# Dividing attention probabilities by their row sums before they are transposed, in a float32 decoder layer on one core

## The reference

```
x = layernorm(x + attention(x))      # 16 heads of 32, softmax over 256 keys, q/k/v/o weights, small 32x32 down/up matrices
x = layernorm(x + x * scan(ctx*ctx)) # scan along the tokens: r = decay*r + ctx*ctx, one decay a head
x = layernorm(x + down(silu(gate(x)) * up(x)))   # hidden 2048; all three weights are splines of few control points
```

```
scores = q @ k.T                              # 256 x 256
p = exp(scores - rowmax) ; rowsum = sum(p)
y = (p / rowsum) @ v
out = concat(y) @ Wo.T
```

## Time and profile before

| | |
|---|---|
| time, median of 3 runs | 684.98 us |
| the profiled execution's own time | 685.51 us |
| its span, first to last instruction | 683.7 us |
| TensorE clock granted, mean | 0.995 |
| PE busy | 656.8 us (96%) |
| DVE busy | 449.5 us (66%) |
| ACT busy | 347.7 us (51%) |
| POOL busy | 294.3 us (43%) |

### The profile page before, as it was taken

One profiled execution on the slowest core, in us unless ns is written; L12 is line 12 of the kernel. 1 busy time (PEld: TensorE's weight loads), 2 busy tenths in 40 slices (PEclk: granted clock), 3 DMA queues, 4 the chain that ended last, 5 costly groups with the idle time before them and its releaser, 6 DMA issues.

```text
span 683.7 us, 12025 instructions
## 1 busy us (share of the span) xinstructions
PE 656.8 (96%) x4312; PEld 533.8 (78%) x4312; DVE 449.5 (66%) x826; ACT 347.7 (51%) x1002; POOL 294.3 (43%) x351
## 2 busy tenths in 40 slices
PE   9999999999999999999988799999999999999993
PEld 9597887878888788788865577888888888888883
DVE  3567687698686877878778688666544555354434
ACT  5566546637466565656667556552334233333230
POOL 1764486886638767594674836100100001000103
PEclk9999999999999999999999999999999999999997
DMA  9621020030220311121112672741193317340301
GB/s 329 221 80 62 1 87 7 2 125 1 94 62 2 133 52 32 63 72 41 40 65 47 159 173 72 210 105 40 35 239 78 81 32 198 72 101 0 124 1 61
DMA packets 22010, 58.06 MB, mean 85 GB/s; under 512 B 4032, under 2 KB 7232, under 8 KB 21056
## 3 DMA queue, kind: packets, MB, share of 16 engines
q1 hardware_dynamic: 16720, 44.45, 22.5%
q0 software_dynamic: 4944, 12.32, 5.9%
q10 hardware_dynamic: 288, 0.52, 0.2%
HBM read 32.11 MB, written 8.39 MB: 59 GB/s over the span
## 4 chain that ended last, share of the span: by engine, by line
PE 78%; DVE 12%; ACT 6%; issue 2%; POOL 1%; DVEq 0%; POOLq 0%; ACTq 0%
PE bank L303 19%; PE bank L305 18%; PE bank L304 18%; PE bank L490 6%; ACT probs L665 5%; PE bank L478 4%; DVE recurrence_T L896 4%; PE bank L512 4%; DVE minus_max L821 3%; PE bank L1191 2%; PE bank L1096 2%; DVE probsT L835 2%; PE bank L529 1%; PE bank L316 1%; PE bank L498 1%
## 5 line engine op out<-in xcount | busy, mean ns | idle before, releaser
L665 ACT ACTIVATE probs<-bank,minus_max 128x256 f32<-128x256 f32 x256 | 117.3, 486 | 23.8 <-DVE minus_max L821 23.8
L303 PE MATMUL bank<-down,hidden_hi_lo 128*128 128x512 f32 x256 | 100.7, 393 | 1.5 <-DVE hidden_hi_lo L1402 1.5
L305 PE MATMUL bank<-down,hidden_hi_lo 128*128 128x512 f32 x256 | 100.5, 392 | 0.0
L304 PE MATMUL bank<-down,hidden_hi_lo 128*128 128x512 f32 x256 | 100.0, 391 | 0.0
L821 DVE TENSOR_REDUCE minus_max<-bank 128x2 f32<-128x512 f32 x128 | 79.3, 681 | 16.3 <-PE bank L478 16.3
L1398 DVE TENSOR_TENSOR hidden<-bank,silu 128x512 f32<-128x512 f32 x64 | 44.1, 689 | 60.9 <-PE bank L305 58.9
L1356 ACT ACTIVATE silu<-bank 128x512 f32<-128x512 f32 x64 | 38.3, 598 | 82.2 <-PE bank L305 81.3
L1402 DVE TENSOR_TENSOR hidden_hi_lo<-hidden,hidden_hi_lo 128x512 fp32r<-128x512 f32 x64 | 45.5, 711 | 40.9 <-ACT hidden_hi_lo L1369 40.8
L490 PE MATMUL bank<-ident,probs 128*128 128x128 f32 x512 | 65.5, 275 | 6.2 <-ACT probs L665 5.9
L1476 POOL TENSOR_TENSOR ffn_var_eps<-ffn_mean_var,constants 128x4 f32<-128x4 f32 x3 | 0.6, 196 | 156.5 <-DVE ffn_mean_var L1418 156.5
L490 PEld LDWEIGHTS bank<-ident,probs 128*128 128x128 f32 x512 | 56.6, 141 | 14.2 <-ACT probs L665 12.0
(11 more groups left out here) (170 smaller groups left out, 1610.8 us busy)
## 6 DMA issues: line engine op xcount, KB each, us to landing
features_by_group<-features_by_cell SPq DMA_DIRECT2D x128, 128.0 KB, 2.4
ctx_squared_T<-in_ctxT SPq DMA_DIRECT2D x8, 512.0 KB, 3.3
xres<-in_x SPq DMA_DIRECT2D x8, 512.0 KB, 4.6
x_in<-x SPq DMA_DIRECT2D x16, 256.0 KB, 3.1
x_residual<-x POOLq DMA_DIRECT2D x4, 1024.0 KB, 8.1
out_x<-x_residual POOLq DMA_DIRECT2D x16, 256.0 KB, 2.8
xin_T<-in_xT SPq DMA_DIRECT2D x7, 512.0 KB, 3.9
x<-x_rows SPq DMA_DIRECT2D x7, 512.0 KB, 4.1
```

Of the source, the lines that this page charges most:

```text
L303: nc.tensor.matmul(out, wh, xh, start=first, stop=False)
L304: nc.tensor.matmul(out, wh, xl, start=False, stop=False)
L305: return nc.tensor.matmul(out, wl, xh, start=False, stop=last)
L665: inc(nc.scalar.activation(probs[:, g, t, :], S[g][:, t * T:(t + 1) * T], ACT.Exp, bias=nmax[:, g, t:t + 1], accum_out=rsum[:, t, g:g + 1] ...
```

## The change

1. The probabilities are divided in rows, right after exp. `dve_inverse` now takes the reciprocal of one head's two row sums as soon as that head's exp is done. ACT multiplies the probabilities of heads 0 to 2 by it in place (six instructions a stage, at the end of `act_exp`), DVE those of head 3 (`dve_weigh`, two instructions). `pe_t` waits for these and not for exp. The spread reciprocal, its transposes (`pe_r`), the copy `Rb`, and the multiplication of y are gone.
2. y stays in MI: ACT rounds it from there to the high part (between exp of heads 2 and 3 of the next stage), DVE subtracts for the low part of every group. GpSimd's share of that is gone.
3. `pe_s` of the next group stands before `pe_pv` of this one.
4. DVE's order in a stage changes, as shown below; the scan of a batch is split into two halves (groups 2 and 3), and batch 7's moves behind the batches, into the transition. `dve_size` moves as well.
5. In the transition, one job more (four, not three) is done ahead of the FFN, recurrence transposes and `act_rs1` come later, and the first FFN step has one job and not two.
6. The last block's normalisation is done by ACT as x*rstd + (-mean*rstd), with GpSimd computing the bias, and SyncE issues the four output DMAs.

The core of the diff:

```diff
@@ pe_t
         for g in range(HG):
-            pe.wait_ge(s["exp"], 32 * b + 8 * m + 2 * g + 2)
+            if g < ON_ACT:
+                pe.wait_ge(s["pna"], ON_ACT * (4 * b + m) + g + 1)
+            else:
+                pe.wait_ge(s["pnv"], (HG - ON_ACT) * (4 * b + m) + g - ON_ACT + 1)
@@ pe_batch, as at every group
-        pe_r(pe, b, 1)
         pe_k(pe, b, 3, rest)
         pe_extra(pe, b, 1)
+
+        pe_s(pe, b, 2)
         pe_pv(pe, b, 1)
-
-        pe_s(pe, b, 2)
@@ act_exp
         for g in range(HG):
+            if m and g == HG - 1:
+                act_yh(act, b, m - 1)
             act.wait_ge(s["max"], 16 * b + 4 * m + g + 1)
             ...
+        for g in range(ON_ACT):
+            act.wait_ge(s["rinv"], 4 * (4 * b + m) + g + 1)
+            for t in range(TT):
+                last = nc.scalar.activation(probs[:, g, t, :], probs[:, g, t, :], ACT.Copy, scale=rinv[:, g, t:t + 1])
+            inc(last, "pna")
@@ dve_y, and dve_yl gone
-        inc(nc.vector.tensor_tensor(y[:], MI[:, 0:T], Rb[:], ALU.mult), "yv")
+        dve.wait_ge(s["yh"], 4 * b + m + 1)
+        inc(nc.vector.tensor_tensor(yT[1][:, m, :], MI[:, 0:T], yT[0][:, m, :].bitcast(F32), ALU.subtract), "yl")
@@ new in DVE
+    def dve_inverse(dve, b, m, g):
+        dve.wait_ge(s["exp"], 32 * b + 8 * m + 2 * g + 2)
+        inc(nc.vector.reciprocal(rinv[:, g, :], rsum[:, g, :]), "rinv")
+
+    def dve_weigh(dve, b, m):
+        for g in range(ON_ACT, HG):
+            dve.wait_ge(s["rinv"], 4 * (4 * b + m) + g + 1)
+            for t in range(TT):
+                last = nc.vector.tensor_scalar(probs[:, g, t, :], probs[:, g, t, :], rinv[:, g, t:t + 1], None, ALU.mult)
+            inc(last, "pnv")
@@ transition, DVE
+            for q, out in enumerate((B_, C_, A_, B_)):
+                dve_fl(dve, 0, q, out)
             dve_job(dve, 2 * NG, X)
+            dve_scan(dve, B - 1, range(KT))
             dve_r1(dve, B - 1, 0)
             dve_job(dve, 2 * NG + 1, X)
+            dve_stats(dve, B - 2, 1)
             dve_r1(dve, B - 1, 1)
             dve_job(dve, 2 * NG + 2, X)
+            dve_job(dve, 2 * NG + 3, X)
@@ end, SyncE
+            for t in range(BT):
+                sp.wait_ge(s["yout"], BT * (NB - 1) + t + 1)
+                inc(sp.dma_start(out_v[:, BT * (NB - 1) + t, :], res[:, t, :]), "last", 16)
```

223 lines of the change are left out of this document (99 added, 124 removed), and 6 rows, old and new, of the table names.

## The result

The changed kernel takes **723.16 us** in the median (four runs, 720.13 to 724.3), beside 685.26 for the kernel before on the same chip: a ratio of 1.0545 (95% interval 1.0528 to 1.0561), 38 us slower. The forecast was 700, with a range of 687 to 709: the side was right, the size was not.

What follows compares the result with a forecast made beforehand. PE set the pace before; after the change VectorE's queue would bind stages 0, 2 and 3, plus batch 7's wait. Terms 6.0 + 1.5 + 0.5 + 6.5 + 2.5 - 2.1 = +14.9 us took 685.0 to 700, range 687 to 709.

Steps and rivals of the forecast that it cites:

- the chain of a stage: Each stage, from its scores' start S: exps end at S+5.8, then the scalings; stage 0 of batches 2 to 7 takes 11.55 us.
- Stage 2 of batch 7: The size reduction there waits for GpSimd ahead of the copies; next scores at S+14.9, the largest single loss expected, 3.9 us.
- stages 2 and 3 of batches 4 to 6: VectorE's scans between its scalings and copies set these stages: 11.15 and 11.75 us, within +6.0 for the three batches.
- step 1: Batches 0 to 3: VectorE's scalings at 0.4 us busy, 0.3 from start to start; +0.5 for batch 0, +1.5 for 1 to 3.
- Rival C: VectorE's scalings are held up by GpSimd, 0.26 us an instruction in 21 stages: +11, 711 us; chance 0.09.
- step 2: ScalarE's six scalings of each stage start 0.30 us apart; stage 1 takes 10.7 with a wait of 0.2 for head 2.
- The condition that I wrote down for it: Sign of a wrong forecast: ScalarE's scalings at 0.45 us, so that PE waits before its transposes, 0.9 a stage.
- step 3: Transition from stage 3's scores in batch 7: VectorE's later queue delays the first down product to S+31.4; +2.5 us net.
- the tail: Last block's normalisation on ScalarE and outputs issued one by one: -2.1 us, bounds -0.9 and -3.3.
- A: PE still sets the pace in all stages: -7.0 for the removed transposes, -2.1 at the end, 676 us; chance 0.12.
- B: Only batch 7 and the transition lose, batches 0 to 6 come out even: +8, 692 us; chance 0.18.
- D: Gains and losses over the whole kernel cancel and 685 us stands; chance 0.03.

## Why the prediction was right or wrong

**Right: the side, the chain of a stage, and its place in stage 0 and in batch 7.** Exps end at S+5.7 (forecast 5.8). Stage 0 with VectorE's statistics behind the scalings is 11.46 (11.55), and it falls to 10.46 when the statistics go ahead of them. Stage 2 of batch 7, with the size reduction behind ScalarE's and GpSimd's queues, is 15.41 (14.9), and the wait for it 5.12 (over 4). PE waited before the scores of stage 1, released by VectorE's copies, but 0.93 and not 1.8.

**Right by luck: stages 2 and 3 of batches 4 to 6.** The forecast put them down to VectorE's queue, 11.15 and 11.75; they are 11.04 and 11.99 in batch 5. But they stay so without VectorE's scalings (11.04, 11.99) and with the scans ahead of them (11.04, 11.98), and fall without ScalarE's (10.70, 11.21). So ScalarE's pace set them. A wrong reason gave nearly the right lengths, and the +6.0 for these batches, measured +7.7, is near in part by this luck.

**Failed step 1, the price of VectorE's scalings in batches 0 to 3.** Forecast +0.5 and +1.5, measured +7.4 and +10.8: 16.2 of the 23.4 us missed. 3.7 of them are the clock (2.8 in batch 0, 0.9 in batch 1, below). I took VectorE's scaling at 0.4 busy and 0.3 from start to start in all batches, although had a mean of 558 ns for L830, whose undisturbed copy takes 295. The runs: without VectorE's scalings batches 0 to 3 take 48.17 and 136.87 instead of 50.77 and 144.17, and about 7.6 of that difference is left when the dips of both executions are set aside. With GpSimd's two kinds of work cut, batches 1 to 3 take 138.5. Rival C named this mechanism and was given 0.09, with 0.26 us excess per instruction. The excess is 0.56 us where GpSimd works (1.73 for a pair instead of 0.61) and 1.0 at worst (2.57), it takes the scans too, and it falls on the batches that I had declared cheapest. My argument against it, that GpSimd waits at those times, holds in stage 0 of batches 2 to 7 and is wrong in stage 2, where GpSimd splits x and multiplies rows. As a sole cause rival C would be wrong too: it is one of two limits. The remaining 5 or so of the 16.2 belong to ScalarE's share, step 2. In batch 0, where no output product covers the chain, stage 0 is 8.66 without divisions and 11.03 with ScalarE's, whether VectorE's are there or not (two executions without a dip in it); the forecast had no term for that.

**Failed step 2, ScalarE's pace.** 0.30 from start to start came from a copy without a scale in the middle of other work; measured 0.40. The forecast had stage 1 at 10.7, with a wait of 0.2; it is 11.0 without VectorE's part, and 11.57 with eight scalings. The condition that I wrote down for it, 0.45 and a wait ahead of the transposes, came out as a stretch between them (2.67 instead of 1.91), which PE's own waits hardly show (11.0 us over the whole run) and those of its weight load do (42.5 us, 90 times).

**Failed step 3, the transition: +2.5 against +10.1.** The path that I followed, VectorE and TensorE up to the first down product, was right: it starts 33.15 after the scores, where I had 31.4, and at 31.50 in the run with throwaway transposes, whose clock there is 0.89 and not 0.57. What I left out is GpSimd's queue of transfers. The size reduction moved one group later, and the makers stand behind it: from silu 10 to silu 20 after takes 53.00, before 47.45, and with the transfers ahead 47.87. So of the 7.6 missed 5.1 are these transfers and 1.7 the clock; 0.8 stay open.

**Missed: the clock.** No term had it. TensorE at 0.50 to 0.84 cost 2.8 us in batch 0 and 0.9 in batch 1 of the profiled execution, and up to 2.7 behind stage 3's scores in batch 7.

**Undersized: the tail.** -3.5 against -2.1, just outside its bounds of -0.9 and -3.3. The sum took the landing of a transfer as equal, whoever starts it; in the traces the last one landed 3.1 us after GpSimd's start and 2.1 after SyncE's. And -1.8 in the FFN from shifted addresses, for which the kernel before gave no sign.

**Rivals A, B and D** fell. A named the work that goes (7.0 for the transposes): without divisions batches 0 to 6 are 10.7 us shorter than before. How much of that is the transposes and how much the earlier scores, no run separates; the divisions cost four times as much. B and D had batches 0 to 6 even; they lost 25.9.

## What to carry to other kernels

When a small amount of TensorE's work, here a pair of transposes a stage, is replaced by element work on two other engines, price that work in two ways: the mean with a busy neighbour, not the undisturbed duration, and the start-to-start time of a run of the same instruction. Remove suspects singly and together; if the two single gains do not add up to the joint one, each hides a part of the other. And when an instruction moves, follow what stands behind it in every queue it shares with others, the transfers on GpSimd and ScalarE's copies included. A stage that comes out as forecast is no proof of its reason: here stages 2 and 3 came out near the forecast for another reason.

## What the runs showed of the hardware

- VectorE's tensor_scalar of 128x256 in SBUF takes 0.34 to 0.35 us with GpSimd quiet and up to 1.42 beside it; a scan of that shape 0.66 and up to 1.78 (after's 64 and 32). The Trainium skill, "SBUF — State Buffer", section "Who interferes with whom", has both: VectorE's two-port operations, and those with two inputs from SBUF against a GpSimd instruction that reads SBUF, wait for the shared pair; the traces agree (2.57 for 0.62 and 3.22 for 1.27).
- ScalarE's scaled copy of 128x256 from SBUF to SBUF goes at 0.40 us from start to start in a run of six, 0.547 each by itself.
- TensorE's granted clock stood at 0.50 (1.2 GHz) in all three 5 us windows from 385 to 400, around waits of 3.6, 4.7 and 3.7 us, and in part of the windows on either side (0.82 and 0.63). In batch 0 a dip came in one execution and not in another of the same code. With a wait of 2.2 us in a stage, as in the kernel with one more piece ahead of the transposes, the clock over the stage was 0.88.
- SyncE's four output transfers, started one by one, end the run 3.0 us sooner than GpSimd's four in a row.
- Sixteen bytes more a partition ahead of the FFN's tiles make its steps 1% shorter (4.13 to 4.08 us) with no instruction changed. Which tile it is, and why, stays open.
